# A graph-and-expert kernel on one core: the logits and sums of each chunk of edges split into small steps that run between the picks

## The chip, the cores and the metric

The kernel runs on one core of one Trainium2 chip. The metric is the device time of one execution in microseconds (us), lower is better; runs are given by their median. The engines are TensorE (PE; its weight loads are PEld), VectorE (DVE), ScalarE (ACT), GpSimd (POOL) and SyncE (SP), which here only issues DMAs. Each engine works through its own program in order and waits on semaphores; the shared quantities are SBUF, PSUM (8 banks) and 16 DMA engines.

## The reference, cut to what matters

```python
x = x + gnn(layernorm(x), W, M, src, dst)          # 6250 nodes x 256, 200,000 edges
x = x + ffn(layernorm(x), ...)                      # below
# in ffn: 131,072 edges, HEADS = 4, NUM_EXPERTS = 4, a self loop for each node
h = (x_flat @ W_gat).reshape(M, HEADS, NUM_EXPERTS)
a_src = (h * att_src).sum(-1); a_dst = (h * att_dst).sum(-1)
e = leaky_relu(a_src[src] + a_dst[dst], 0.2)
e_max = segment_max(e, dst); ee = exp(e - e_max[dst]); denom = segment_sum(ee, dst)
agg = segment_sum(h[src] * (ee / denom[dst])[:, :, None], dst)      # 16 numbers a node
scores = layernorm(agg + b_gat).mean over heads; the best 2 of 4 experts gate
out = sum over experts of gate * (gelu(x @ W1[e] + b1[e]) @ W2[e] + b2[e])
```

## The kernel before

The first part (up to about 2230 us) does the first graph layer, sorts the 131,072 edges of the second by destination, and runs most of the experts' matmuls between them. The change lies in the **second edge stage**, about 2269 to 3022 us, and what follows waits for it.

**Edges and chunks.** The sorted edges lie as 1024 columns of 128 partitions, in NCF = 16 chunks of FC = 64 columns. A chunk's buffer `g[:, c % 5]` (GR = 5) holds for each edge 16 features, 4 logits and 4 running maxima. The first PC = 32 columns of a chunk are fetched from `tab_d` by GpSimd: 32 indirect DMAs (L1465), one a column. The other TC = 32 columns are made by TensorE.

**Blocks on TensorE.** 8 blocks (TB) of 4 columns make a chunk's second half, 128 blocks in all. For a block, VectorE writes one-hot rows `low_hot` (L788, 4 instructions; two buffers), TensorE multiplies them with the table in three bf16 parts (L1368, 48 matmuls of 208 columns), and VectorE picks the values out: `picked` (L799) and a reduction into `g` (L804). Block b + 1's one-hot rows wait for block b - 1's matmuls, and TensorE's block b waits for `low_hot` b and for L799 of block b - 2. So TensorE runs at most one block ahead.

**Steps.** `turns_2` sets the order on every engine: "matrix" steps, 4 for each block (516 = 4 x 129 in all), and units of the experts' matmuls that are left (40 of them among the steps: L1314 for a hidden part, L1324 for a y tile, whose bias add L724 is VectorE's). In a block's four steps VectorE does the pick of block b - 1 in the first, the one-hot rows of b + 1 in the second, nothing in the other two.

**Logits and sums.** For chunk c, `weigh(c)` takes the logits: products for the second half (L823, L825), 4 scans that spread the destination's number along the row (L839), a wait for the chunk's 32 gathers (`feat_in`), sum and leaky relu (L846, L847), 4 scans for running maxima (L849), differences (L855 to L858). ScalarE takes exponentials (`exps`). `sum_up(c)` multiplies (L864, L867) and runs 20 scans of 64 columns (L871). In the kernel before, `weigh(c)` runs as a whole after step 32 (c + 1.5) and `sum_up(c)` as a whole after step 32 (c + 1.75). Chunk 15's two run behind the last step.

**GpSimd** runs 32 gathers for chunk 0, 49 scatters of the destinations' numbers into `start_d` (`starts`, L1454), then the gathers of chunks 1 to 15. From chunk 5 on it waits for `summed` of chunk c - 4 and for the store of chunk c - 5.

**SP** waits for all 49 scatters before it loads the first three chunks of `edge` from `start_d` (at step 32), stores a y tile after each y unit, stores a chunk's sums to `sum_d` (L1639) after `sum_up`, and behind the last step issues 15 loads of `comb` (L1676, L1677; 896 KB each) and then the last chunk's sums. When those have landed, GpSimd fetches the rows' last sums (L1473), mends them, and fetches 49 tiles of sums; the gates and the weighted sum of the experts end the kernel.

Of the kernel before, what the change touches and what calls it, by code (L numbers as in the profile page):

```python
# [33 lines left out]
CR = 3  # L34
PART = 3
POOL_TILES = 2


class Steps:
# [16 lines left out]
def sent(k):  # L56

    return 16 * (k + 1)


def build(nc, x, src, dst, W, M, W_gat, att_src, att_dst, b_gat, ln_gamma, ln_beta,
# [3 lines left out]
    NX, _, F = W1.shape  # L65
# [22 lines left out]
    NCF = C2 // FC  # L88
    PC = FC - TC
    NTC = NCF * TC  # L90
    TB = TC // 4
# [194 lines left out]
    def sem(name):  # L286
        if name not in named:
            named[name] = nc.alloc_semaphore(name)
        return named[name]
# [28 lines left out]
    for j in range(V_):  # L318
        paced += PACE if j >= 2 * JC else 0
        n = min(int(paced), sort_total - taken_steps) if j % 2 else 0  # L320
# [35 lines left out]
    for j in range(V_):  # L356
        paced = min(paced + (SEARCH_PACE if search_from <= j <= search_end else UNIT_PACE), 2.0)
        n = 0
        if j % 2 and paced >= 1 and units_1 < len(units):
            what, i, _ = units[units_1]  # L360
            first = y_from if what == "y" else (ready(last_of(jobs[i][0])) + UNIT_WAIT) * JC
            if j >= first:
                n, units_1, paced = 1, units_1 + 1, paced - 1
# [13 lines left out]
    matrix_total = 4 * (NCF * TB + 1)  # L377
# [4 lines left out]
        turns_2 += ["unit"] * int(paced) + ["matrix"]  # L382
        paced -= int(paced)
    turns_2 += ["unit"] * (left - turns_2.count("unit"))
    weigh_at = {int(4 * TB * (c + 1.5)): c for c in range(NCF - 1)}
    sum_at = {int(4 * TB * (c + 1.75)): c for c in range(NCF - 1)}
    low_at = {4 * TB * (c + 1) + 2: c + 2 for c in range(NCF - 2)}

    def vector_program():
        step = Steps(V, dve_step)  # L390

        def then(ins):
            n = step(ins)
            V.wait_ge(dve_step, n)
            return n
# [114 lines left out]
        for b in range(VB + 1):  # L510
# [3 lines left out]
            if b >= 1:  # L514
                V.wait_ge(sem("pairs_turned"), b)
                at = slice((b - 1) * P, b * P)
# [289 lines left out]
        def matrix_gathers():  # L806
            split_table()
            low_columns(0)
            for b in range(NCF * TB + 1):
                if b >= 1:  # L810
                    pick(b - 1)
                yield
                if b + 1 < NCF * TB:
                    low_columns(b + 1)
                yield
                yield
                yield

        def scores(c):

            s = c % GR
            V.wait_ge(dve_step, dve_at["pick", (c + 1) * TB - 1])
            then(V.tensor_tensor(scored[:, :, :], g[:, s, PC:FC, 0:HX],  # L823
                                 attb[:, 0:1, :].broadcast_to([P, TC, HX]), ALU.mult))
            step(V.tensor_reduce(g[:, s, PC:FC, HX:FE], scored[:, :, :].rearrange("p k (h e) -> p k h e", h=HEADS),  # L825
                                 AXX, ALU.add))

        def weigh(c):
            a, b, s, e = c * FC, (c + 1) * FC, c % GR, c % 4
            e_, top_, st = g[:, s, :, HX:FE], g[:, s, :, FE:FG], step_f[:, c % 2, :, :]  # L830
            before_top = None if c == 0 else g[:, (c - 1) % GR, FC - 1:FC, FE:FG]
            a_dest, same = edge[:, e, :, :], same_f[:, a:b]
            scores(c)
            V.wait_ge(sem(f"edge_in{e}"), sent(c // 4))
            if c == 0:
                V.wait_ge(sem("row_in"), 16)
                then(V.tensor_copy(a_dest[:, 0, :], head_row[:, FE:FG]))
            for f in range(HEADS):
                step(V.tensor_tensor_scan(a_dest[:, :, f], same, a_dest[:, :, f],  # L839
                                          0.0 if c == 0 else edge[:, (c - 1) % 4, FC - 1:FC, f], ALU.mult, ALU.add))  # L840
            if c >= 2:
                V.wait_ge(dve_step, dve_at["summed", c - 2])
            step(V.tensor_scalar(reset_c[:, c % 2, :], same, -1.0, BIG, ALU.add, ALU.mult))
            V.wait_ge(sem(f"feat_in{s}"), 16 * PC * (c // GR + 1))
            step.settle()
            then(V.tensor_tensor(e_, e_, a_dest, ALU.add))  # L846
            then(V.scalar_tensor_tensor(out=e_, in0=e_, scalar=0.2, in1=e_, op0=ALU.mult, op1=ALU.max))  # L847
            for h in range(HEADS):
                step(V.tensor_tensor_scan(g[:, s, :, FE + h], reset_c[:, c % 2, :], g[:, s, :, HX + h],  # L849
                                          -BIG if c == 0 else before_top[:, :, h], ALU.add, ALU.max))  # L850
            step.settle()
            if c == 0:
                step(V.memset(st[:, 0:1, :], -BIG))
            else:
                step(V.tensor_tensor(st[:, 0:1, :], before_top, top_[:, 0:1, :], ALU.subtract))  # L855
            step(V.tensor_tensor(st[:, 1:FC, :], top_[:, 0:FC - 1, :], top_[:, 1:FC, :], ALU.subtract))
            then(V.tensor_tensor(e_, e_, top_, ALU.subtract))
            dve_at["weighed", c] = then(V.tensor_scalar(st, st, 0.0, None, ALU.min))  # L858

        def sum_up(c):  # L860
            a, b, s = c * FC, (c + 1) * FC, c % GR
            st = step_f[:, c % 2, :, :]
            V.wait_ge(sem("exps"), c + 1)
            step(V.tensor_tensor(st, st, same_f[:, a:b, None].broadcast_to([P, FC, HEADS]), ALU.mult))  # L864
            for h in range(HEADS):
                o = g[:, s, :, h * NX:(h + 1) * NX]
                step(V.tensor_tensor(o, o, g[:, s, :, HX + h:HX + h + 1].broadcast_to([P, FC, NX]), ALU.mult))  # L867
            step.settle()
            for f in range(FE):
                h = f // NX if f < HX else f - HX  # L870
                step(V.tensor_tensor_scan(g[:, s, :, f], st[:, :, h], g[:, s, :, f],  # L871
                                          0.0 if c == 0 else g[:, (c - 1) % GR, FC - 1:FC, f], ALU.mult, ALU.add))
            dve_at["summed", c] = step.settle()

        matrix_steps, done = matrix_gathers(), 0
        for turn in turns_2:
            if turn == "unit":
                next(mlp)
                continue
            next(matrix_steps)  # L880
            done += 1
            if done in weigh_at:
                weigh(weigh_at[done])
            if done in sum_at:
                sum_up(sum_at[done])
        for _ in mlp:
            pass
        weigh(NCF - 1)

        cm = sm[:, 20:20 + HEADS]  # L890
        w = hm[:, 0, :, :]
        dve_at["tops_spread"] = then(V.tensor_tensor(
            w, ident[:, None, :].broadcast_to([P, HEADS, P]),
            g[:, (NCF - 1) % GR, FC - 1, FE:FG, None].broadcast_to([P, HEADS, P]), ALU.mult))
        sum_up(NCF - 1)
        V.wait_ge(sem("tops_out"), 1)
        then(V.tensor_tensor(w, bank[0][:, :].rearrange("p (h q) -> p h q", h=HEADS),
                             segm[:, 0:1, :].broadcast_to([P, HEADS, P]), ALU.mult))
# [87 lines left out]
        for c in range(NLN):  # L986
# [6 lines left out]
            for e in range(NX):  # L993
                for k in range(XG - POOL_TILES):
                    step(V.scalar_tensor_tensor(  # L995
# [5 lines left out]
    def scalar_program():  # L1001
# [120 lines left out]
        def exps(c):  # L1122
            st, e_ = step_f[:, c % 2, :, :], g[:, c % GR, :, HX:FE]
            A.wait_ge(dve_step, dve_at["weighed", c])
            A.activation(st, st, ACT.Exp)
            A.activation(e_, e_, ACT.Exp).then_inc(sem("exps"), 1)

        done = 0
        for turn in turns_2:
            if turn == "unit":  # L1130
                next(mlp)
                continue
            done += 1
            if done in weigh_at:
                exps(weigh_at[done])
        exps(NCF - 1)
        w = hm[:, 0, :, :]
        A.wait_ge(dve_step, dve_at["carry_logit"])
# [19 lines left out]
        for c in range(NLN):  # L1158
# [5 lines left out]
            for e in range(NX):  # L1164
                for k in range(XG - POOL_TILES, XG):
                    y = comb[:, s, e, k, :]
# [330 lines left out]
    def sync_program():  # L1497
# [78 lines left out]
        for c in range(NCH + AFTER):  # L1576
# [10 lines left out]
            if c == LOW_CH:  # L1587
                Q.wait_ge(dve_step, dve_at["low_rows"])
                for k in range(LB):
                    n = min(P, NTC - k * P)  # L1590
# [17 lines left out]
            if size(c):  # L1608
                n = size(c)
# [12 lines left out]
        def load_edges(c):  # L1622
            if c >= 4:
                Q.wait_ge(dve_step, dve_at["weighed", c - 3])
            Q.dma_start(edge[:, c % 4, :, :].rearrange("p j f -> p (j f)"),
                        start_d.rearrange("(p j) f -> p (j f)", p=P)[:, c * FC * HEADS:(c + 1) * FC * HEADS]
                        ).then_inc(sem(f"edge_in{c % 4}"), 16)
# [9 lines left out]
        def store_sums(c):  # L1637
            Q.wait_ge(dve_step, dve_at["summed", c])
            Q.dma_start(sum_rows[:, c * FC:(c + 1) * FC, :], g[:, c % GR, :, :]).then_inc(sem(f"sum_out{c % GR}"), 16)  # L1639
# [4 lines left out]
        done = 0  # L1644
        for turn in turns_2:
            if turn == "unit":
                next(mlp)
                continue
            done += 1
            if done == 4 * TB:  # L1650
                Q.wait_ge(sem("start_out"), 16 * NT)
                for c in range(3):
                    load_edges(c)
            if done in low_at:
                load_low(low_at[done])
            if done in weigh_at and weigh_at[done] + 3 < NCF:
                load_edges(weigh_at[done] + 3)
            if done in sum_at:
                store_sums(sum_at[done])
        for _ in mlp:  # L1660
            pass
        for k in range(2):
# [19 lines left out]
        for c in range(NLN):  # L1682
# [3 lines left out]
            n = min(XG, FULL // P - c * XG)  # L1686
# [38 lines left out]
```

## Time and profile before

| what | us |
|---|---|
| median of 3 runs | 3240.63 (3239.18 to 3240.84) |
| the profiled execution | 3242.23, its span 3240.9 |
| TensorE's first and last matmul of the stage (L1368) | 2269.2, 3022.0 |
| GpSimd's gathers of chunks 1 to 15 | 2340.4 to 2999.3 |
| first `comb` load issued; last sums landed | 3027.0; 3071.8 |
| from there to the end | 169.1 |

The profile's span is 1.3 us less than the profiled execution's time, and that time is 1.6 us over the median. In the profile each row of a timeline is a run of like instructions on one engine: its start, how long it took, the count, and in brackets for how long the engine was idle before it and what released it.

### The profile page before, as it was taken

How to read it: one execution, taken by the hardware profiler on the slowest of the kernel's cores; microseconds unless marked ns; L12 is line 12 of the kernel's file. 1: busy time of each engine (PE TensorE's matmuls, PEld its weight loads, DVE VectorE, ACT ScalarE, POOL GpSimd, SP SyncE). 2: the span in 40 equal slices, each digit the busy share in tenths (PEclk: the TensorE clock that was granted, in tenths of full speed). 3: DMA queues.
4: the chain of work that ended last, by engine and by line, in shares of the span. 5: the costliest groups of instructions: out<-in, count | busy, mean ns of one | idle time of the engine just before them, and what ended most of it. 6: DMA issues, size and time to landing. Idle time of an engine off the chain costs nothing.

```text
span 3240.9 us, 41199 instructions
## 1 busy us (share of the span) xinstructions
PE 2411.0 (74%) x13096; PEld 1894.9 (58%) x13096; DVE 2192.3 (68%) x5126; ACT 543.2 (17%) x924; POOL 2331.4 (72%) x2315
## 2 busy tenths in 40 slices
PE   1466878878778888788888888886888888888300
PEld 0344555556556555566666666664788887888200
DVE  6488777678685656565556555553588888888568
ACT  4000212112123333211111111111000000000012
POOL 3777777777777777777777777774777777777073
PEclk9777999889889989899999999898999999999655
DMA  8876777667767777777777777774122122211518
GB/s 277 297 226 218 221 224 226 216 214 230 218 208 243 239 223 238 223 223 236 232 247 246 239 235 238 234 237 131 26 62 62 39 61 62 55 44 44 192 43 270
DMA packets 470542, 599.63 MB, mean 185 GB/s; under 512 B 66293, under 2 KB 409270, under 8 KB 468278
## 3 DMA queue, kind: packets, MB, share of 16 engines
q1 hardware_dynamic: 372310, 375.12, 34.9%
q0 software_dynamic: 97568, 220.03, 24.6%
q8 instruction: 105, 1.72, 0.2%
q10 hardware_dynamic: 448, 1.85, 0.2%
q14 instruction: 111, 0.91, 0.1%
HBM read 312.22 MB, written 286.19 MB: 185 GB/s over the span
## 4 chain that ended last, share of the span: by engine, by line
PE 32%; DVE 16%; DMA 9%; issue 6%; POOL 5%; SPq 3%; ACT 1%; DVEq 0%; POOLq 0%; ACTq 0%
PE wide L1266 9%; PE wide L1368 9%; PE wide L1324 5%; PE wide L1314 5%; DMA run_d<-ring 4%; DVE g L871 2%; DMA fetched<-x_d 2%; DVE ring L746 2%; DVE low_hot L788 2%; DVE comb L995 2%; DVE picked L799 2%; PE wide L1283 2%; POOL ring L1438 1%; POOL start_d L1454 1%; DMA ring<-xn_d,srci 1%
## 5 line engine op out<-in xcount | busy, mean ns | idle before, releaser
L1438 POOL DMA_INDIRECT ring<-xn_d,srci x1611 | 1623.4, 1008 | 516.7 <-issue 443.6
L746 DVE SCALAR_TENSOR_TENSOR ring<-ring,same_v,wide 128x256 f32<-128x256 f32 x1610 | 770.6, 479 | 694.8 <-PE wide L1266 588.0
L1266 PE MATMUL wide<-ring,one_hot 128*128 128x256 f32 x3222 | 916.8, 421 | 164.5 <-DVE ring L746 95.1
L1266 PEld LDWEIGHTS wide<-ring,one_hot 128*128 128x128 f32 x3222 | 652.7, 211 | 377.8 <-DVE ring L746 132.6
L1368 PE MATMUL wide<-tab_parts,low_hot 128*128 128x208 bf16 x6144 | 599.9, 263 | 120.2 <-DVE low_hot L788 120.2
L1368 PEld LDWEIGHTS wide<-tab_parts,low_hot 128*128 128x128 bf16 x6144 | 576.4, 102 | 145.5 <-DVE low_hot L788 128.4
L1465 POOL DMA_INDIRECT g<-tab_d,srt x512 | 547.2, 1069 | 156.0 <-issue 154.2
L1324 PE MATMUL wide<-w2s,hh 128*128 128x256 f32 x1568 | 390.1, 394 | 2.3 <-DVE yo L724 2.3
L1314 PE MATMUL wide<-xt,w1s 128*128 128x512 f32 (+1 forms) x832 | 390.8, 594 | 0.8 <-DVE feat L714 0.8
L1324 PEld LDWEIGHTS wide<-w2s,hh 128*128 128x128 f32 x1568 | 311.7, 200 | 56.0 <-issue 6.1
L1079 ACT ACTIVATE hh<-wide,b1c 128x512 f32<-128x512 f32 (+1 forms) x208 | 137.8, 663 | 1218.2 <-PE wide L1314 1217.9
L682 DVE TENSOR_TENSOR one_hot<-iota_f,dloc 128x512 f32<-128x512 f32 x403 | 276.5, 687 | 3.1
L1314 PEld LDWEIGHTS wide<-xt,w1s 128*128 128x128 f32 x832 | 162.4, 202 | 113.5 <-issue 99.1
L799 DVE TENSOR_TENSOR picked<-wide,high_hot 128x832 f32<-128x832 f32 x128 | 130.8, 1022 | 106.7 <-PE wide L1368 105.7
L1274 PE MATMUL wide<-ident,fetched 128*128 128x128 f32 x196 | 46.0, 378 | 182.4 <-DMA fetched<-x_d 182.4
L788 DVE TENSOR_SCALAR low_hot<-low_row,lane 128x512 bf16<-128x512 f16 x512 | 157.0, 369 | 0.0
L1274 PEld LDWEIGHTS wide<-ident,fetched 128*128 128x128 f32 x196 | 29.8, 187 | 205.1 <-DMA fetched<-x_d 204.7
L804 DVE TENSOR_REDUCE g<-picked 128x64 f32<-128x832 f32 x128 | 130.6, 1020 | 4.4
L724 DVE TENSOR_TENSOR yo<-wide,b2b 128x256 f32<-128x256 f32 x196 | 82.0, 418 | 46.8 <-PE wide L1324 45.6
L607 DVE TENSOR_TENSOR keys<-keys 128x512 f32<-128x512 f32 (+1 forms) x198 | 112.2, 567 | 0.0
L606 DVE TENSOR_TENSOR keys<-keys 128x512 f32<-128x512 f32 (+1 forms) x198 | 111.8, 565 | 0.0
L1095 ACT ACTIVATE tin<-wide 128x512 f32<-128x512 f32 x49 | 29.2, 597 | 461.4 <-PE wide L1274 461.4
(332 smaller groups left out, 1569.8 us busy)
## 6 DMA issues: line engine op xcount, KB each, us to landing
run_d<-ring SPq DMA_DIRECT2D x201, 1024.0 KB, 5.3
ring<-xn_d,srci POOLq DMA_INDIRECT x1611
y_d<-yo SPq DMA_DIRECT2D x196, 128.0 KB
comb<-y_d SPq DMA_DIRECT2D x28, 896.0 KB, 9.6
low_row<-low_d SPq DMA_DIRECT2D x16, 1024.0 KB, 5.6
sum_d<-g SPq DMA_DIRECT2D x16, 768.0 KB, 3.3
g<-tab_d,srt POOLq DMA_INDIRECT x512
xn_d<-ring SPq DMA_DIRECT2D x7, 896.0 KB, 5.6
```

What stands on the lines that cost most here:

```text
L682: dve_at["one_hot", b] = step(V.tensor_tensor(one_hot[:, b % 4, 0:n, :], iota_f[:, None, :].broadcast_to([P, n, P]), dloc[:, 4 * b:4 * b + ...
L746: dve_at["run", j] = step(V.scalar_tensor_tensor(out=o, in0=ring[:, (j - 1) // JC % RING, (j - 1) % JC, :], scalar=same_v[:, j:j + 1], in1 ...
L788: dve_at["low_hot", b] = step(V.tensor_scalar(low_hot[:, b % 2, q_, :], low_row[:, c % 2, at:at + LOW], lane[:, q_:q_ + 1], None, ALU.is_e ...
L799: dve_at["taken", b] = then(V.tensor_tensor(picked[:, :, :, :], wide[:, 4 + half:6 + half, :].rearrange("p c (k x) -> p (c k) x", k=2)[:, ...
L804: dve_at["pick", b] = step(V.tensor_reduce(g[:, c % GR, k:k + 4, 0:HX], picked[:, :, :, :], AXX, ALU.add))
L1079: A.activation(hh[:, i % 2, f, 0:n * P], bank[hidden_bank[nl]][:, 0:n * P], ACT.Gelu, bias=b1c[:, e, f:f + 1], scale=1.0).then_inc(sem("ge ...
L1266: T.matmul(wide[:, 4 + j // 2 % 2, j % 2 * D:(j % 2 + 1) * D], one_hot[:, j // 4 % 4, j % 4, :], ring[:, j // JC % RING, j % JC, :], start ...
L1314: mm = T.matmul(bank[hidden_bank[nl]][:, 0:n * P], w1s[:, e, k, f * P:(f + 1) * P], xt[:, c % 2, k, 0:n * P], start=(k == 0), stop=(k == K ...
L1324: mm = T.matmul(bank[y_bank[ny]][:, 0:D], hh[:, i % 2, k, f * P:(f + 1) * P], w2s[:, e, k, :], start=(k == 0), stop=(k == KF - 1))
L1368: mm = T.matmul(bank[4 + 2 * (b % 2) + i // 2][:, at:at + HX * HI], low_hot[:, b % 2, q_, i * P:(i + 1) * P], tab_parts[:, k, q_, :, :].re ...
L1438: G.indirect_dma_start(out=ring[:, s, j % JC, :], out_offset=None, in_=xn_d, in_offset=at_rows(srci[:, j:j + 1])).then_inc(sem(f"gather{s} ...
L1465: G.indirect_dma_start(out=g[:, s, k, :], out_offset=None, in_=tab_d, in_offset=at_rows(srt[:, j:j + 1])).then_inc(sem(f"feat_in{s}"), 16)
```

## The change

`weigh` and `sum_up` become generators. `weigh(c)` yields 9 times and `sum_up(c)` 13 times; the 20 scans are in 10 pieces of 2. A new generator, `chunk_steps`, runs through chunks 0 to 14 with 29 steps each (CHUNK_STEPS): 9 for the logits, 4 empty ones, 13 for the sums, 3 empty ones. From step 89 on (first_weigh = 88) each matrix step of VectorE advances it by one. The instructions, their number and their operands stay the same. Chunk 0's logits so begin 40 steps later than before, chunk 14's at step 495 where it was 496. The last steps of chunk 14's sums lie behind step 516, and run ahead of chunk 15. ScalarE's exponentials, SP's loads of `edge` and its stores of sums move with them; SP's wait for the scatters moves from step 32 to step 84, and chunk 14's store behind its loop.

```diff
+CHUNK_STEPS = 29
+WEIGH_STEPS = 9
+EXP_STEPS = 4
+SUMMED_STEPS = 28
...
-    weigh_at = {int(4 * TB * (c + 1.5)): c for c in range(NCF - 1)}
-    sum_at = {int(4 * TB * (c + 1.75)): c for c in range(NCF - 1)}
+    first_weigh = 4 * TB * 11 // 4
+    weighed_at = {first_weigh + CHUNK_STEPS * c + WEIGH_STEPS: c for c in range(NCF - 1)}
+    summed_at = {first_weigh + CHUNK_STEPS * c + SUMMED_STEPS: c for c in range(NCF - 1)}
...
             for f in range(HEADS):
                 step(V.tensor_tensor_scan(a_dest[:, :, f], same, a_dest[:, :, f],
                                           0.0 if c == 0 else edge[:, (c - 1) % 4, FC - 1:FC, f], ALU.mult, ALU.add))
+                if f % 2:
+                    yield
...
             for h in range(HEADS):
+                if h % 2 == 0:
+                    yield
                 step(V.tensor_tensor_scan(g[:, s, :, FE + h], reset_c[:, c % 2, :], g[:, s, :, HX + h],
...
             for f in range(FE):
+                if f % 2 == 0:
+                    yield
                 h = f // NX if f < HX else f - HX
                 step(V.tensor_tensor_scan(g[:, s, :, f], st[:, :, h], g[:, s, :, f],
                                           0.0 if c == 0 else g[:, (c - 1) % GR, FC - 1:FC, f], ALU.mult, ALU.add))
             dve_at["summed", c] = step.settle()
-
-        matrix_steps, done = matrix_gathers(), 0
+            yield
+
+        def chunk_steps():
+
+            for c in range(NCF - 1):
+                n = 0
+                for _ in weigh(c):
+                    n += 1
+                    yield
+                assert n <= WEIGH_STEPS
+                for _ in range(WEIGH_STEPS + EXP_STEPS - n):
+                    yield
+                n = WEIGH_STEPS + EXP_STEPS
+                for _ in sum_up(c):
+                    n += 1
+                    yield
+                assert n <= SUMMED_STEPS
+                for _ in range(CHUNK_STEPS - n):
+                    yield
...
             next(matrix_steps)
             done += 1
-            if done in weigh_at:
-                weigh(weigh_at[done])
-            if done in sum_at:
-                sum_up(sum_at[done])
+            if done > first_weigh:
+                next(chunks, None)
         for _ in mlp:
             pass
-        weigh(NCF - 1)
+        for _ in chunks:
+            pass
+        for _ in weigh(NCF - 1):
+            pass
...
-            if done == 4 * TB:
+            if done == first_weigh - 4:
                 Q.wait_ge(sem("start_out"), 16 * NT)
                 for c in range(3):
                     load_edges(c)
...
-            if done in weigh_at and weigh_at[done] + 3 < NCF:
-                load_edges(weigh_at[done] + 3)
-            if done in sum_at:
-                store_sums(sum_at[done])
+            if done in weighed_at and weighed_at[done] + 3 < NCF:
+                load_edges(weighed_at[done] + 3)
+            if done in summed_at:
+                store_sums(summed_at[done])
+        for at, c in summed_at.items():
+            if at > matrix_total:
+                store_sums(c)
```

VectorE in the middle of the stage, one chunk's sums, before: L799, L804 and L788 are a block's pick and one-hot rows, L864, L867 and L871 the sums (the scans are printed as SCALAR_TENSOR_TENSOR here).

```order
L799 TENSOR_TENSOR picked<-wide,high_hot 128x832
L804 TENSOR_REDUCE g<-picked 128x4x16
L788 TENSOR_SCALAR low_hot<-low_row,lane 128x512 x4
L864 TENSOR_TENSOR step_f<-step_f,same_f 128x256
L867 TENSOR_TENSOR g<-g 128x64x4 x4
L871 SCALAR_TENSOR_TENSOR g<-step_f,g 128x64 x20
L799 TENSOR_TENSOR picked<-wide,high_hot 128x832
```

The same place now; the line numbers are those of the changed kernel (L805, L810 and L794 are the pick and the one-hot rows, L879, L885 and L891 the sums).

```order
L794 TENSOR_SCALAR low_hot<-low_row,lane 128x512 x4
L891 SCALAR_TENSOR_TENSOR g<-step_f,g 128x64 x6
L805 TENSOR_TENSOR picked<-wide,high_hot 128x832
L810 TENSOR_REDUCE g<-picked 128x4x16
L891 SCALAR_TENSOR_TENSOR g<-step_f,g 128x64 x2
L794 TENSOR_SCALAR low_hot<-low_row,lane 128x512 x4
L891 SCALAR_TENSOR_TENSOR g<-step_f,g 128x64 x6
```

The 25 instructions of the sums stood together between two blocks; now at most 6 scans stand between two instructions of a block.

SP, the first loads of `edge` (L1625) among the loads of `low_row` (L1632), the first sums (L1639) and the y tiles (L1571), before:

```order
L1571 DMA y_d<-yo 128x256
L1625 DMA edge<-start_d 128x256 x3
L1632 DMA low_row<-low_d 128x4096
L1625 DMA edge<-start_d 128x256
L1570 TENSOR_LOAD tiles_i
L1570 ISA x2
L1571 ISA
L1571 DMA y_d<-yo 128x256
L1639 DMA sum_d<-g 128x1536
```

And now (L1666, L1673, L1680 and L1612 are the same four):

```order
L1612 DMA y_d<-yo 128x256
L1673 DMA low_row<-low_d 128x4096
L1611 TENSOR_LOAD tiles_i
L1611 ISA x2
L1612 ISA
L1612 DMA y_d<-yo 128x256
L1666 DMA edge<-start_d 128x256 x4
L1673 DMA low_row<-low_d 128x4096
```

The loads of `edge`, which stand behind the wait for the scatters, moved behind two loads of `low_row` and two y tiles.

## Rows read from the trace of the kernel before

**Rows 1.** The page: busy time of each engine, and the gathers' group.

```profile
PE 2411.0 (74%) x13096; PEld 1894.9 (58%) x13096; DVE 2192.3 (68%) x5126; ACT 543.2 (17%) x924; POOL 2331.4 (72%) x2315
...
L1465 POOL DMA_INDIRECT g<-tab_d,srt x512 | 547.2, 1069 | 156.0 <-issue 154.2
```

**Rows 2.** Busy time by stretch; then PEclk, DMA share and GB/s.

```profile
2397.80:2401.20 3.40, 3.40 (x23) 3.01 (x21) 3.37 (x9) 0.00 (x0) 2.54 (x3) 0.51 0.10 11
2343.60:3022.00 678.40, 579.40 (x5713) 551.50 (x5714) 565.67 (x1335) 59.34 (x82) 510.37 (x478) 0.92 0.22 54
```

**Rows 3.** Waits in the stage: us in total, times, longest.

```profile
PE wide L1368 <- DVE low_hot L788: 120.2, 31, 16.6
DVE picked L799 <- PE wide L1368: 105.7, 66, 6.3
```

**Rows 4.** Timeline of TensorE around chunk 1's logits and sums.

```profile
2370.48 14.07 PE L1368 MATMUL wide<-tab_parts,low_hot 128*128 128x208 bf16 x156
2384.39 1.91 PE L1324 MATMUL wide<-w2s,hh 128*128 128x256 f32 x8
2386.14 7.65 PE L1368 MATMUL wide<-tab_parts,low_hot 128*128 128x208 bf16 x84
2396.92 8.25 PE L1368 MATMUL wide<-tab_parts,low_hot 128*128 128x208 bf16 x72 [3.13 <-DVE low_hot L788]
```

**Rows 5.** Timeline of VectorE, chunk 1's logits, sums and next blocks.

```profile
2387.72 0.68 DVE L823 TENSOR_TENSOR scored<-g,attb 128x512 f32<-128x512 f32 x1
...
2393.41 0.29 DVE L858 TENSOR_SCALAR step_f<-step_f 128x256 f32<-128x256 f32 x1
2393.74 1.02 DVE L799 TENSOR_TENSOR picked<-wide,high_hot 128x832 f32<-128x832 f32 x1
...
2400.00 0.47 DVE L864 TENSOR_TENSOR step_f<-step_f,same_f 128x256 f32<-128x256 f32 x1
...
2401.84 5.82 DVE L871 TENSOR_TENSOR_SCAN g<-step_f,g 128x64 f32<-128x64 f32 x20
2407.70 1.02 DVE L799 TENSOR_TENSOR picked<-wide,high_hot 128x832 f32<-128x832 f32 x1
2408.76 1.02 DVE L804 TENSOR_REDUCE g<-picked 128x64 f32<-128x832 f32 x1
...
2410.74 1.02 DVE L799 TENSOR_TENSOR picked<-wide,high_hot 128x832 f32<-128x832 f32 x1
```

**Rows 6.** Timeline of GpSimd over the same scans.

```profile
2402.59 1.02 POOL L1465 DMA_INDIRECT g<-tab_d,srt  x1 [0.30 <-issue]
2403.92 4.57 POOL L1465 DMA_INDIRECT g<-tab_d,srt  x1 [0.30 <-issue]
2408.80 0.94 POOL L1465 DMA_INDIRECT g<-tab_d,srt  x1 [0.30 <-issue]
2410.05 1.07 POOL L1465 DMA_INDIRECT g<-tab_d,srt  x1 [0.30 <-issue]
```

**Rows 7.** Timeline of GpSimd, over the start of chunk 8's sums.

```profile
2728.09 1.84 POOL L1465 DMA_INDIRECT g<-tab_d,srt  x1 [0.31 <-issue]
```

**Rows 8.** Timeline of GpSimd: last scatter, first and last gather of chunks 1 to 15, fetch.

```profile
2339.16 0.98 POOL L1454 DMA_INDIRECT start_d<-feat,idx_s  x1 [0.30 <-issue]
2340.44 1.00 POOL L1465 DMA_INDIRECT g<-tab_d,srt  x1 [0.31 <-issue]
...
2998.26 1.07 POOL L1465 DMA_INDIRECT g<-tab_d,srt  x1 [0.30 <-issue]
3071.82 0.94 POOL L1473 DMA_INDIRECT sm<-sum_d,smi  x1 [72.49 <-DMA sum_d<-g]
```

**Rows 9.** Timeline of VectorE: chunk 0's logits.

```profile
2343.56 0.40 DVE L837 COPY edge<-head_row 128x4 f32<-128x4 f32 x1 [14.55 <-DMA edge<-start_d]
```

**Rows 10.** Timeline of SP's queue behind the last block.

```profile
3027.01 4.75 SPq L1676 DMA_DIRECT2D comb<-y_d  x4
...
3060.66 2.54 SPq L1639 DMA_DIRECT2D sum_d<-g  x1
```

More of the change, by code:

```diff
@@ L384, in build @@
     turns_2 += ["unit"] * (left - turns_2.count("unit"))
-    weigh_at = {int(4 * TB * (c + 1.5)): c for c in range(NCF - 1)}
-    sum_at = {int(4 * TB * (c + 1.75)): c for c in range(NCF - 1)}
+    first_weigh = 4 * TB * 11 // 4
+    weighed_at = {first_weigh + CHUNK_STEPS * c + WEIGH_STEPS: c for c in range(NCF - 1)}
+    summed_at = {first_weigh + CHUNK_STEPS * c + SUMMED_STEPS: c for c in range(NCF - 1)}
+    assert first_weigh + CHUNK_STEPS * (NCF - 2) + WEIGH_STEPS < matrix_total
     low_at = {4 * TB * (c + 1) + 2: c + 2 for c in range(NCF - 2)}
@@ L864, in sum_up @@
             step(V.tensor_tensor(st, st, same_f[:, a:b, None].broadcast_to([P, FC, HEADS]), ALU.mult))
+            yield
             for h in range(HEADS):
+                if h == 2:
+                    yield
                 o = g[:, s, :, h * NX:(h + 1) * NX]
@@ L869, in sum_up @@
             for f in range(FE):
+                if f % 2 == 0:
+                    yield
                 h = f // NX if f < HX else f - HX
@@ L873, in sum_up @@
             dve_at["summed", c] = step.settle()
-        matrix_steps, done = matrix_gathers(), 0
+            yield
+        def chunk_steps():
[3 more added lines that the diff above has]
+                    n += 1
+                    yield
+                assert n <= WEIGH_STEPS
+                for _ in range(WEIGH_STEPS + EXP_STEPS - n):
+                    yield
+                n = WEIGH_STEPS + EXP_STEPS
+                for _ in sum_up(c):
+                    n += 1
+                    yield
+                assert n <= SUMMED_STEPS
+                for _ in range(CHUNK_STEPS - n):
+                    yield
+        matrix_steps, chunks, done = matrix_gathers(), chunk_steps(), 0
         for turn in turns_2:
@@ L894, in vector_program @@
             g[:, (NCF - 1) % GR, FC - 1, FE:FG, None].broadcast_to([P, HEADS, P]), ALU.mult))
-        sum_up(NCF - 1)
+        for _ in sum_up(NCF - 1):
+            pass
         V.wait_ge(sem("tops_out"), 1)
@@ L1133, in scalar_program @@
             done += 1
-            if done in weigh_at:
-                exps(weigh_at[done])
+            if done in weighed_at:
+                exps(weighed_at[done])
         exps(NCF - 1)
```

## The prediction

> **What bounds the kernel now.** I read the page first: over the whole span no engine is full, TensorE is busy 74% of it, VectorE 68%, GpSimd 72% [rows 1], so the stage has to be read by itself. In the stage TensorE needs 13.91 us for 156 matmuls (14.07 with the last one's own length; the next matmuls start at 2384.39) [rows 4], that is 4.28 us for a block's 48. VectorE needs 3.04 us for a block's pick and one-hot rows (2407.70 to 2410.74) [rows 5]. So between the chunks' work TensorE sets the pace and VectorE has 1.24 us to spare in a block, which is why the picks wait for TensorE 105.7 us in all [rows 3]. Then come the logits, 6.02 us in one piece (2387.72 to 2393.74), and the sums, 7.70 us in one piece (2400.00 to 2407.70) [rows 5]. TensorE runs at most one block ahead, so each piece stops it: 31 waits for the one-hot rows, 120.2 us in all, 3.9 us on average, 16.6 the longest [rows 3]. The longest is chunk 0's, whose logits wait 14.55 us for the first `edge` load behind the 49 scatters [rows 9]. A stop also costs clock: after one of 3.13 us [rows 4] a stretch of 3.4 us was granted 0.51 of the clock, the lower of its two levels (1.2 of 2.4 GHz), and held 23 matmuls [rows 2], where at full level 38 would fit. Over the stage the clock is 0.92 [rows 2].
>
> The second bound lies close behind. GpSimd never waits in this stage, but for 0.3 us of issue before each gather (156.0 over 512 [rows 1]): its gathers of chunks 1 to 15 run from 2340.44 to 2999.3 [rows 8], 658.9 us or 43.9 a chunk. Its pitch without trouble is 1.25 us a gather (2408.80 to 2410.05 [rows 6]), 40.0 a chunk; so 3.9 a chunk are delays, 3.6 of them in one gather. That one stands in every chunk's 20 scans: 4.57 us where 0.94 is usual, and it ends 0.83 us behind the last scan [rows 5, 6]. Before, a chunk's 32 steps took about 47 us, more than GpSimd's 43.9, so its rows were always there in time. TensorE's last matmul ended at 3022.0, GpSimd at 2999.3: only 22.7 us lie between them.
>
> Last, the way out. Behind the last block SP issues the `comb` loads from 3027.01, its queue takes the last sums at 3060.66, and they have landed at 3071.82, when GpSimd goes on [rows 8, 10]: 44.8 us from first load to landing. All of the remaining 169.1 us follow from there.
>
> **The change part by part.** *What goes.* With at most 6 scans between two of a block's instructions, TensorE's waits shrink. Per interval of 29 steps (7.25 blocks) TensorE needs 7.25 x 4.28 = 31.0 us and its share of the 40 units (0.31 a block, 1.76 us each from 2384.39 to 2386.14 [rows 4]: 3.9), 34.9 in all. VectorE needs 7.25 x 3.04 + 6.02 + 7.70 = 35.8. Since the pieces stand in 22 of 29 steps, VectorE is a little late there and idle elsewhere; I take 37 us. Without GpSimd the steps would cost 37 a chunk.
>
> *What is late next.* GpSimd needs 40 + x a chunk, x being its delays, which is more than 37. Step 88 comes at about 2269 + 22 blocks x 4.8 us (4.28 and the units) = 2375, chunk 0's logits then find edges and rows there, and its 14.55 us wait is gone. From there the steps reach chunk c's logits at 2378 + 37 c, while its gathers are there at 2340 + (40 + x) c + 2. For x near 1.3 the two cross at chunk 8; from then on VectorE waits inside the logits for the gathers, in front of the picks and one-hot rows that are queued behind that wait, and TensorE waits for those. So the pace is GpSimd's, and the end is computed from it.
>
> *The sum.* x: the small delays of today, 43.9 - 40 - 3.5 = 0.4, stay. The long one depends on how scans keep GpSimd out. The gather that starts 0.75 us into the 20 scans takes 1.02 us, 0.08 too much; only the one that starts 2.08 us in is caught [rows 5, 6]. Six scans last 1.73 us (5.82 less 5.82/20 for each left out), so runs of the new length lie wholly in the part that lets gathers through. Against this stands one gather of 1.84 us near a start of the sums [rows 7], 0.9 too much, which I found in 3 of the 14 chunks with smaller ones. I price each of a chunk's three or four runs at 0.08 plus a fifth of 0.9, some 0.9 together, and take x = 1.3.
> Gathers of chunk 14 are then there at 2340.4 + 14 x 41.3 + 2 = 2920.6. From its fourth logit step VectorE still has 18 steps, 4.5 blocks x 3.04 = 13.7 us, and 3.7 us of logits and 7.7 of sums: 25 us, so its sums end at 2946. SP can then issue the `comb` loads at about 2947, and one store of sums (2.5 us in the queue [rows 10]) stands ahead of them. The last sums land at 2947 + 2.5 + 44.8 = 2994.3, against 3071.8: 77.5 us less. Chunk 15 is hidden: its gathers are there at 2340.4 + 15 x 41.3 + 2 = 2961.9, logits, spread and sums take 12 to 13 us more, 2975, and the queue reaches its store only at 2983. The rest is unchanged. The profiled execution's 3242.2 less 77.5 is 3164.7; the median stands 1.6 below that execution, so 3163.
>
> *Costed at nothing.* No instruction is added. ScalarE's exponentials have four empty steps (over 4 us) for 0.8 us of work. SP's wait for the scatters (the last starts at 2339.16 [rows 8]) is moved to step 84, at about 2370, past two `low_row` loads and two y stores, which it no longer holds up. Chunk 5's gathers wait for chunk 1's sums at about 2440, and start at 2505. If any of these covers failed, the price would be a stop such as those of today, 3.9 us each.
>
> *A rule.* The scans read two SBUF operands. Back to back, they let two gathers through at 1.02 us and then none [rows 6]. The Trainium skill (SBUF — State Buffer, Who interferes with whom) says that a VectorE instruction with two SBUF inputs contends with a GpSimd instruction that reads SBUF, as a lock for the whole instruction; taken at its word each piece of scans could hold up a gather wherever it stands, which is the third rival below.
>
> **The rivals.** (1) *The same starvation.* The scans' total is the same, and the low_hot instructions beside them may count as part of a run. Then x stays 3.9: chunk 14's gathers are there 2.6 x 14 = 36.4 us later, 3200. The ends of the long gather, 4.57, at any chunk [rows 6] speak for a fixed amount of blocking; the two that pass speak against it.
> (2) *VectorE stays the bound.* If pieces between picks cost as many stops as before, the steps keep some 45 us a chunk and only the first wait (14.55) goes: about 3225. Against it: the sum of VectorE's work is 35.8.
> (3) *Slower: every piece of scans catches a gather*, as in the 1.84 us row [rows 7]. Ten pieces at 0.9 make x = 9.4; the last sums land 8.1 x 14 = 113 us later than in my sum, 3277. It decides from x = 1.3 + 77.5/14 = 6.8 on, 0.64 us for each piece. Against it stand the gathers that pass between scans [rows 6].
> (4) *Slower: the clock.* TensorE's waits become short and frequent. If it stood at the lower level for half of the blocks, a block would cost the mean of 4.28 and twice that, 6.4 us, 129 blocks and 70 us of units 896 against 753 now, some 140 slower, 3380. The dip shown follows a stop of 3.1 us, and such stops become rare, against it.
>
> **How the numbers follow.** My forecast has 63%, and by itself x from 0.4 to about 2.5: 3150 to 3180, with 5 us for gathers that land later while the `comb` loads fill the DMA engines. Rival 1 has 20% (3180 to 3212), rival 2 6%, rival 3 7%, rival 4 4%. The range 3145 to 3210 takes in most of the first two. A measurement of this kernel tells 0.2%, 6.5 us, from no change. Faster by more: 0.88; within: 0.03; slower: 0.09.
>
> **What the profile would show.** Right: no gather over 2 us in the scans, GpSimd's last gather of the stage near 2960, waits of VectorE inside the logits (the sum of g and edge, L846 before) that begin at about chunk 8, TensorE's waits more in number and mostly under 2 us, the first `comb` load near 2950 and the fetch of the last sums near 2994, 169 us before the end. Rival 1 shows in the gathers' end at 2999 and waits for gathers from chunk 1 or 2 on. Wrong altogether would be gathers of 1.8 us at every piece, or a mean clock under 0.8 in the stage.

## The result, and the profile after

The changed kernel takes **3158.17 us** (median of 4 runs, 3153.76 to 3162.35) where the kernel before takes 3240.74 (4 runs): a ratio of 0.9745, interval 0.9728 to 0.9762, some 82.6 us less. The profiled execution took 3162.35, its span is 3161.0. L805, L810, L794, L1409, L1506 are what L799, L804, L788, L1368, L1465 were.

The page's two groups of the stage, TensorE's matmuls and GpSimd's gathers (count, busy us, mean ns, idle before and its releaser), against 599.9 busy and 120.2 waited on TensorE, and the 547.2 of [rows 1]:

```profile
L1409 PE MATMUL wide<-tab_parts,low_hot 128*128 128x208 bf16 x6144 | 573.3, 255 | 62.2 <-DVE low_hot L794 61.8
L1506 POOL DMA_INDIRECT g<-tab_d,srt x512 | 506.4, 989 | 156.1 <-issue 153.6
```

The stage, first matmul 2269.8 to last 2934.7, is 664.9 us long where it was 752.8. Busy time of each engine from chunk 0's old stop on, and then PEclk, against [rows 2], where that stretch had 0.92:

```profile
2343.60:2934.70 591.10, 541.23 (x5622) 515.83 (x5620) 549.12 (x1301) 60.63 (x83) 451.06 (x460) 0.99 0.24 59
```

The waits in the stage, against [rows 3]:

```profile
PE wide L1409 <- DVE low_hot L794: 61.8, 47, 12.4
...
DVE picked L805 <- PE wide L1409: 39.2, 28, 6.3
...
DVE g L855 <- DMA g<-tab_d,srt: 14.5, 6, 4.6
```

TensorE waits for the one-hot rows more often and for less: 61.8 us here, 58.4 less. 12.4 of it, as of the 120.2 before, is the wait for the stage's very first rows. The picks wait 39 us for TensorE, no longer 106: VectorE is now the busier of the two (549 of 591 us). New is the last line, VectorE inside the logits waiting for gathers. The rest of the gain is the matmuls themselves, 599.9 to 573.3 us busy, 26.6 less, since the clock of the stretch is 0.99: behind its first microseconds it falls only after the four stops of 2.5 to 4.9 us, where before it fell after most of the stops. 58.4 and 26.6 are 85 of the stage's 87.9.

GpSimd, first and last gather of chunks 1 to 15 and the fetch of the last sums, against [rows 8]:

```profile
2341.13 1.00 POOL L1506 DMA_INDIRECT g<-tab_d,srt  x1 [0.30 <-issue]
...
2958.22 0.94 POOL L1506 DMA_INDIRECT g<-tab_d,srt  x1 [0.30 <-issue]
2992.72 0.94 POOL L1514 DMA_INDIRECT sm<-sum_d,smi  x1 [33.56 <-DMA sum_d<-g]
```

618.1 us for 15 chunks, 41.2 each where it was 43.9. SP behind the last block, against [rows 10]:

```profile
2942.11 0.32 SPq L1680 DMA_DIRECT2D sum_d<-g  x1
2942.75 6.44 SPq L1720 DMA_DIRECT2D comb<-y_d  x4
...
2981.69 2.54 SPq L1680 DMA_DIRECT2D sum_d<-g  x1
```

Chunk 14's sums are stored at 2942.11, `comb` follows at once, and the fetch comes at 2992.72, 168 us before the span's end (it was 169).

### The profile page after: what moved, and what is told of

Its sections match the earlier page's. It is cut to its first block and busy times, and to the rows that moved or that the text cites. A ratio compares the mean times of both kernels' runs of the same rounds, so it can differ in the third digit from the quotient of the medians.

```text
span 3161.0 us, 41206 instructions
## 1 busy us (share of the span) xinstructions
PE 2382.3 (75%) x13096; PEld 1866.7 (59%) x13096; DVE 2190.1 (69%) x5126; ACT 543.4 (17%) x924; POOL 2290.7 (72%) x2315
## 5 line engine op out<-in xcount | busy, mean ns | idle before, releaser
L1409 PE MATMUL wide<-tab_parts,low_hot 128*128 128x208 bf16 x6144 | 573.3, 255 | 62.2 <-DVE low_hot L794 61.8
L1506 POOL DMA_INDIRECT g<-tab_d,srt x512 | 506.4, 989 | 156.1 <-issue 153.6
L1409 PEld LDWEIGHTS wide<-tab_parts,low_hot 128*128 128x128 bf16 x6144 | 551.8, 99 | 85.4 <-DVE low_hot L794 75.4
L1315 PE MATMUL wide<-ident,fetched 128*128 128x128 f32 x196 | 44.8, 370 | 176.1 <-DMA fetched<-x_d 176.1
L805 DVE TENSOR_TENSOR picked<-wide,high_hot 128x832 f32<-128x832 f32 x128 | 130.3, 1018 | 40.3 <-PE wide L1409 39.2
L794 DVE TENSOR_SCALAR low_hot<-low_row,lane 128x512 bf16<-128x512 f16 x512 | 157.5, 369 | 0.8
L810 DVE TENSOR_REDUCE g<-picked 128x64 f32<-128x832 f32 x128 | 130.6, 1020 | 4.4
```

The lines of the kernel that those rows point to most:

```text
L794: dve_at["low_hot", b] = step(V.tensor_scalar(low_hot[:, b % 2, q_, :], low_row[:, c % 2, at:at + LOW], lane[:, q_:q_ + 1], None, ALU.is_e ...
L805: dve_at["taken", b] = then(V.tensor_tensor(picked[:, :, :, :], wide[:, 4 + half:6 + half, :].rearrange("p c (k x) -> p (c k) x", k=2)[:, ...
L810: dve_at["pick", b] = step(V.tensor_reduce(g[:, c % GR, k:k + 4, 0:HX], picked[:, :, :, :], AXX, ALU.add))
L1409: mm = T.matmul(bank[4 + 2 * (b % 2) + i // 2][:, at:at + HX * HI], low_hot[:, b % 2, q_, i * P:(i + 1) * P], tab_parts[:, k, q_, :, :].re ...
L1506: G.indirect_dma_start(out=g[:, s, k, :], out_offset=None, in_=tab_d, in_offset=at_rows(srt[:, j:j + 1])).then_inc(sem(f"feat_in{s}"), 16)
```

## The experiments

But for the chip at the end of this section, the runs are from chips where the kernel before takes 3240 to 3242 us (medians); the medians of the changed kernels are of 4 or 5 runs.

**1. The 20 scans whole.** Everything stays split and moved but the scans.

```diff
             for f in range(FE):
-                if f % 2 == 0:
+                if f == 0:
                     yield
```

> The changed kernel with one part undone: the 20 scans of a chunk's sums stand in one piece again; all else stays split. Theory A (GpSimd's gathers set the end of the stage, and a run of 20 scans starves them): one gather of about 4.5 us a chunk comes back, the gathers of chunks 1 to 15 take about 43.9 us a chunk instead of 41.2, chunk 14's are there about 38 us later, and the time is about 3195 (3185 to 3205). Theory B (the pace is set by TensorE and VectorE; GpSimd is not the limit): only one more stop of TensorE of about 4 us a chunk, partly made up in the empty steps, at most 3175.

Measured: 3206.2 us (ratio 0.9886, 0.9862 to 0.991), 1 us above Theory A's range and far from Theory B's. GpSimd's gathers of the 15 chunks (busy us, mean ns), and one of the long ones, which are there again in each chunk from 1 on:

```profile
L1506 POOL DMA_INDIRECT g<-tab_d,srt x480 | 513.1, 1069 | 146.3 <-issue 143.8 <-DVE picked L805 0.6 <-DVE g L891 0.6
```

```profile
2608.76 4.58 POOL L1506 DMA_INDIRECT g<-tab_d,srt  x1 [0.30 <-issue]
```

They end at 3000.3, 43.9 a chunk, and the fetch of the last sums comes at 3034.62, 42 us later than in the changed kernel. So 10 pieces of two scans instead of one of 20 are worth about 48 of the 83 us.

The time is Theory A's, but the wait is not. VectorE's timeline shows no wait for gathers in chunks 1 to 14: its logits take up chunk 14's gathers 5.3 us after they have ended, without a pause.

```profile
2955.29 0.94 POOL L1506 DMA_INDIRECT g<-tab_d,srt  x1 [0.30 <-issue]
```

```profile
2961.56 0.44 DVE L855 TENSOR_TENSOR g<-g,edge 128x256 f32<-128x256 f32 x1
```

The steps themselves had become slower, as Theory B has it: the sums of chunks 0 to 14 end 41.1 us apart. The stage is 704.5 us long against 664.9, and of these 39.6 us TensorE's waits for the one-hot rows make 25.7 (87.5 against 61.8) and its matmuls 13.1 (586.4 us busy against 573.3, at a clock of 0.95 against 0.98 over the whole stage). But chunk 14's gathers end 38.7 us later than in the changed kernel, which waits for them, so faster steps alone would have won back at most some 4 us. The two limits lie that close together here, and this run can't say how much of the 48 us is due to either. The whole scans without the scatters would tell; that was not run.

**2. Moved but not split.**

```diff
-                n = 0
-                for _ in weigh(c):
-                    n += 1
-                    yield
-                assert n <= WEIGH_STEPS
-                for _ in range(WEIGH_STEPS + EXP_STEPS - n):
-                    yield
-                n = WEIGH_STEPS + EXP_STEPS
-                for _ in sum_up(c):
-                    n += 1
-                    yield
+                for _ in range(WEIGH_STEPS - 1):
+                    yield
+                for _ in weigh(c):
+                    pass
+                yield
+                for _ in range(EXP_STEPS + 12):
+                    yield
+                for _ in sum_up(c):
+                    pass
+                yield
+                n = WEIGH_STEPS + EXP_STEPS + 13
```

> The changed kernel with the logits and the sums of a chunk each in one piece again, but at the new places (29 steps a chunk, the logits at the ninth of them, the first at step 97). It tells the moving from the splitting. Theory A (the splitting carries the gain; moving takes only chunk 0's wait of 14.55 us away): TensorE's waits for the one-hot rows stay near 105 us, time 3220 to 3240. Theory B (the late start carries it): about 3175.

Measured: 3276.46 us (ratio 1.01, 1.0078 to 1.0121). Both theories missed: moving alone is not worth little, it costs 34 us. Its waits, and its longest stop but the first in TensorE's timeline:

```profile
PE wide L1409 <- DVE low_hot L794: 140.3, 30, 12.4
```

```profile
2559.96 4.33 PE L1409 MATMUL wide<-tab_parts,low_hot 128*128 128x208 bf16 x24 [6.62 <-DVE low_hot L794]
```

And what VectorE did before that, from the reduction of a pick to the next one-hot rows:

```profile
2550.16 1.02 DVE L810 TENSOR_REDUCE g<-picked 128x64 f32<-128x832 f32 x1
2551.10 0.41 DVE L879 TENSOR_TENSOR step_f<-step_f,same_f 128x256 f32<-128x256 f32 x1
2551.43 1.42 DVE L885 TENSOR_TENSOR g<-g 128x256 f32<-128x256 f32 x4
2552.89 5.82 DVE L891 TENSOR_TENSOR_SCAN g<-step_f,g 128x64 f32<-128x64 f32 x20
2558.75 1.16 DVE L794 TENSOR_SCALAR low_hot<-low_row,lane 128x512 bf16<-128x512 f16 x4
```

The sums stand between a block's pick and its one-hot rows, since 29 steps are no multiple of 4: TensorE, one block ahead at most, waits for nearly all of the 7.7 us. Chunk 0's long wait is gone, but the 29 stops behind the very first cost 4.4 us on average; in the kernel before the 29 stops other than the very first and chunk 0's cost 3.1.

**3. The same with 28 steps a chunk**, each piece behind a fourth step.

```diff
-CHUNK_STEPS = 29
+CHUNK_STEPS = 28
-SUMMED_STEPS = 28
+SUMMED_STEPS = 25
-    first_weigh = 4 * TB * 11 // 4
+    first_weigh = 4 * TB * 11 // 4 + 3
-                for _ in range(EXP_STEPS + 12):
+                for _ in range(EXP_STEPS + 11):
-                n = WEIGH_STEPS + EXP_STEPS + 13
+                n = WEIGH_STEPS + EXP_STEPS + 12
```

> whole_late (logits and sums each in one piece at new places, 3276 us, where 3220 to 3240 had been expected) with 28 steps a chunk instead of 29, so that every piece stands behind a block's fourth step as in the kernel before, the first at step 100. Theory A (in whole_late the pieces wander through the block's steps, and one that stands behind the first step, between the pick and the one-hot rows, costs TensorE 5.0 to 6.6 us where the others cost 2.5 to 4): no stop over 5.2 us behind the first, stops of 3.5 us on average as before, 105 to 110 us in all, time 3235 to 3260. Theory B (what costs is that two pieces come every 29 steps instead of every 32, at a time when nothing else is different): 3275 or more.

Measured: 3254.99 us (ratio 1.005, 1.0031 to 1.0068), 21 less than in experiment 2, within Theory A's time but not with its stops. Its waits are

```profile
PE wide L1409 <- DVE low_hot L794: 127.5, 30, 12.4
```

115.1 us in 29 stops behind the first, 4.0 each, five of them at 5.4 to 5.9, where none over 5.2 was expected. So the place in the block is part of the matter (4.4 to 4.0, none at 6.6 any more), but not all: 3.5 was expected, and the kernel before has 3.1. Why whole pieces cost more here than where they stood before stays open.

**4. Split but not moved.**

```diff
-CHUNK_STEPS = 29
+CHUNK_STEPS = 32
-    first_weigh = 4 * TB * 11 // 4
+    first_weigh = 4 * TB * 3 // 2 - 1
-            if done == first_weigh - 4:
+            if done == 4 * TB:
```

> The changed kernel with the splitting alone: chunk 0's logits begin at step 48 as in the kernel before, 32 steps a chunk, the loads of edge behind the wait for the scatters at step 32 again. Theory A (the stage's end is set by chunk 14's gathers, which don't depend on when the logits begin): chunk 0's wait of about 12 to 15 us comes back but is made up before chunk 11, time 3155 to 3165. Theory B (the late start is worth its wait): about 3172.

Measured: 3165.64 us (ratio 0.977, 0.9743 to 0.9797; the changed kernel's interval, 0.9728 to 0.9762, overlaps it), just above Theory A's range. The waits:

```profile
PE wide L1409 <- DVE low_hot L794: 67.4, 51, 12.4
...
DVE g L855 <- DMA g<-tab_d,srt: 12.6, 6, 3.6
DVE edge L844 <- DMA edge<-start_d: 12.6, 1, 12.6
```

Chunk 0's wait for the first edges is back, 12.6 us, and the waits for gathers are 12.6 where they were 14.5: from the middle of the stage both kernels wait for the same gathers. In its profiled execution the first matmul is at 2263.5 and the fetch of the last sums at 2989.56, 726.1 us later; in the changed kernel 722.9. So the late start with 29 steps a chunk instead of 32 brings 3 us in the traces, up to 7 in the medians, not told from none, and the splitting carries the rest.

**5. Without the scatters.** It leaves out the destinations' share of the logits.

```diff
-            for t in range(NT):
-                G.indirect_dma_start(out=start_d, out_offset=at_rows(idx_s[:, t:t + 1]), in_=feat[:, t, FE:FG],
-                                     in_offset=None, bounds_check=E2 - 1,
-                                     oob_is_err=False).then_inc(sem("start_out"), 16)
...
-                Q.wait_ge(sem("start_out"), 16 * NT)
```

> The changed kernel without GpSimd's 49 scatters of the destinations' numbers into start_d (that part of the computation is left out: the destinations' share of the logits is zero but for a row's head). GpSimd has 63 us less to do ahead of chunk 1's gathers. Theory A (from about chunk 11 on the stage waits for GpSimd): VectorE's waits for gathers vanish, the steps keep 37 us a chunk to the end, chunk 14's sums end about 20 us earlier, time 3130 to 3142. Theory B (TensorE and VectorE set the pace to the end): 3155 to 3160 as with the scatters.

Measured: 3133.44 us (ratio 0.9665, 0.964 to 0.969), Theory A. No wait for gathers is left and TensorE's are

```profile
PE wide L1409 <- DVE low_hot L794: 49.7, 49, 12.4
```

with chunk 14's sums stored at 2917.79 and a granted clock of 1.00 over the stage (behind its first microseconds no stretch at the lower level). The changed kernel is thus held some 25 us by GpSimd; here, with the gathers begun 68 us earlier, the sums end 36.4 us apart up to chunk 14.

**6. Two runs of ten scans**, a block apart.

```diff
             for f in range(FE):
-                if f % 2 == 0:
+                if f == 0:
                     yield
+                if f == 10:
+                    for _ in range(4):
+                        yield
```

> The changed kernel with the 20 scans in two runs of 10 (2.9 us each), a block apart. Theory A (in runs of 20 the first two gathers passed and only one that started over 1.8 us in was caught, until the end): longest gathers about 1.7 us where the 20 gave 4.6, 41 to 42 us for a chunk's gathers, time 3160 to 3175. Theory B (a lock held in proportion to the scans' total time, whatever their runs): 43 us and more a chunk, 3190.

Measured: 3180.52 us (ratio 0.9816, 0.9795 to 0.9836), between the times of the two theories. Gathers take 42.9 a chunk (chunks 1 to 14, 2335.8 to 2936.7) and 9 of them 3.1 us. One of these, and VectorE around it:

```profile
2439.60 0.94 POOL L1509 DMA_INDIRECT g<-tab_d,srt  x1 [0.31 <-issue]
2440.85 3.10 POOL L1509 DMA_INDIRECT g<-tab_d,srt  x1 [0.30 <-issue]
2444.26 0.94 POOL L1509 DMA_INDIRECT g<-tab_d,srt  x1 [0.30 <-issue]
```

```profile
2438.19 1.02 DVE L810 TENSOR_REDUCE g<-picked 128x64 f32<-128x832 f32 x1
2439.12 1.13 DVE L794 TENSOR_SCALAR low_hot<-low_row,lane 128x512 bf16<-128x512 f16 x4
2440.17 2.96 DVE L894 TENSOR_TENSOR_SCAN g<-step_f,g 128x64 f32<-128x64 f32 x10
2443.16 1.02 DVE L805 TENSOR_TENSOR picked<-wide,high_hot 128x832 f32<-128x832 f32 x1
```

The gather starts only 0.68 us into the scans, where I had expected it to pass, but 1.73 us after the start of the four one-hot instructions, which the scans follow without a gap. It ends 0.82 us behind the last scan. I looked at the gathers over 1.3 us behind the scatters, of this trace (24) and of the changed kernel's (7): each started 1.7 to 2.7 us after the start of such an unbroken run of one-hot, product and scan instructions, and ended 0.8 us behind the run, whether a pick ended it or VectorE's pause of some 0.04 us between the products and the scans. So the one-hot instructions ahead of the scans count too, and the length of the scans alone doesn't tell.

But a start that late is not enough. Of the gathers that started 1.7 us or more into such a run, with 0.5 us or more of it left, 24 of 35 were held here, and only 7 of 37 in the changed kernel; the others took at most 1.3 us. Here is one that passed, 2.34 us into a run of the same 4 one-hot instructions and 10 scans, with 1.69 us of it left:

```profile
2435.54 1.08 POOL L1509 DMA_INDIRECT g<-tab_d,srt  x1 [0.30 <-issue]
```

```profile
2433.20 1.15 DVE L794 TENSOR_SCALAR low_hot<-low_row,lane 128x512 bf16<-128x512 f16 x4
2434.28 2.95 DVE L894 TENSOR_TENSOR_SCAN g<-step_f,g 128x64 f32<-128x64 f32 x10
```

What tells the held ones from those that pass is open, and so is what it is in a pick or a pause that lets a held gather go. All this is read from traces; none of it was tried by itself.

**7. The last sums before the third group of `comb`.**

```diff
-        for c in range(CR):
+        for c in range(CR - 1):
             load_comb(c)
         store_sums(NCF - 1)
+        load_comb(CR - 1)
```

> The changed kernel as the measure for tail_b in this call, since the call before it ran on a chip where TensorE was fed one matmul in 2.8 us for stretches of the trace: 3155 to 3165 if this chip is like the first.

> The changed kernel, but SP issues two groups of comb loads, then the last chunk's sums, then the third group. Theory A (the store's landing behind the comb loads sets the rest): it lands 8 to 9 us earlier than in the changed kernel (2991.8 in its first trace), and the time is 8 to 9 us less than after_b. Theory B (the third group of loads is needed as early, or the store shares the queue anyway): within 2 us of after_b. On the slow chip the order gave 4347 against 4376, too far apart in its stalls to be read.

Measured on one chip: the changed kernel 3158.47 us (5 runs, 3145.77 to 3161.48), the other order 3152.1 (5 runs, 3150.92 to 3161.05; ratio to the kernel before 0.974 and 0.9743, with intervals of 0.002 to each side). It is the fastest median of a kernel that computes all, and not told from the changed kernel. GpSimd from the fetch of the last sums to the first of the 49 fetches, first in the changed kernel (its sums were made at 2961.4), then in the other (2969.9):

```profile
2978.16 0.94 POOL L1514 DMA_INDIRECT sm<-sum_d,smi  x1 [33.31 <-DMA sum_d<-g]
2982.87 1.02 POOL L1517 DMA_INDIRECT sum_d<-sm,smi  x1 [3.77 <-DVE sm L960]
2985.29 0.97 POOL L1522 DMA_INDIRECT fsum<-sum_d,idx_f  x1 [1.40 <-DMA sum_d<-sm,smi]
```

```profile
2975.32 0.94 POOL L1514 DMA_INDIRECT sm<-sum_d,smi  x1 [22.62 <-DMA sum_d<-g]
2983.30 1.02 POOL L1517 DMA_INDIRECT sum_d<-sm,smi  x1 [7.03 <-DVE sm L960]
2988.18 0.97 POOL L1522 DMA_INDIRECT fsum<-sum_d,idx_f  x1 [3.87 <-DMA sum_d<-sm,smi]
```

The sums land 5.4 us after they are made, no longer 16.8; but from there to the first of the 49 fetches it is 12.9 us instead of 7.1, for the two small DMAs now run beside the third group: the DMA engines are 100% busy in these 12.9 us and 3% in the other kernel's 7.1. Of some 11 us won, half is given back. Theory A's earlier landing is there, but the medians lie only 6.4 us apart, and the runs of the two kernels overlap, so no gain is shown.

**Another chip.** The same order, the ten-scan kernel and the order with a later start also ran on a slower chip:

> tail_order with the logits begun 8 steps later (first_weigh 96). Theory A (the steps wait for GpSimd from about chunk 11 on, so a later start lets TensorE finish first): TensorE's last matmul about 8 us earlier, but the last chunk's sums hang on GpSimd's last gather as before, so the time is within 2 us of tail_order. Theory B (the lag costs, since more sums stand behind the last step): 3 to 6 us slower than tail_order.

On that chip the kernel before took 4459 us, the changed kernel 4376, this one 4359, the other order alone 4347, the ten-scan kernel 4391. For the changed kernel I had expected the time of the first chip, 3155 to 3162. Its ratio there is 0.9807 (0.976 to 0.9853), so it is faster there too. For stretches of over 100 us TensorE started one matmul in 2.80 us, though nothing in the profile held it:

```profile
3016.83 0.33 PE L1409 MATMUL wide<-tab_parts,low_hot 128*128 128x208 bf16 x1 [2.47 <-issue]
3019.63 0.33 PE L1409 MATMUL wide<-tab_parts,low_hot 128*128 128x208 bf16 x1 [2.47 <-issue]
```

The idle time put down to issue before L1409 is 424.1 us there. The runs of one kernel lie up to 55 us apart there, so differences of a few us between kernels mean nothing, and whether a later lag still helps stays open.

## Why the prediction was right, step by step

Predicted 3163, measured 3158.2.

- **TensorE's stops** shrink as forecast: mostly about 1 us, 45 with the first, the longest behind it 4.9. That VectorE's and TensorE's own pace would be 37 us a chunk was right: the sums of chunks 0 to 9 end at 2413.5 to 2747.2, 37.1 each; without the scatters the steps keep it to the end (36.4).
- **What is late next** was named rightly. GpSimd's 41.3 a chunk were 41.2; VectorE waits for gathers in the logits from chunk 9 on, where chunk 8 had been worked out. Experiment 5 shows it: 25 us earlier with gathers begun 68 us earlier. Experiment 1, with slower gathers, ends 42 us later but shows it only in part, since there the steps themselves are as slow.
- **The sum**, term by term: chunk 14's rows there at 2920.6, measured 2919.1 (the start of the instruction that waits for them); its sums' end at 2946, measured 2942.1; the first `comb` load at 2947, measured 2942.8; the landing at 2994.3, measured 2992.7. That the last agrees so well is partly luck: the store ahead of the loads held the queue for 0.6 us and not 2.5, and from the first load to the landing it was 50.0 us and not 44.8. Of the 5 us between 3163 and 3158.2, 2.6 are the profiled execution against the median: it lay 1.6 above the median before and 4.2 above it now.
- **x = 1.3**, the one term that was chosen and not read, was 1.2, for a partly wrong reason. I had argued that six scans are too short a run. But six gathers of chunks 1 to 14 took 1.34 to 1.95 us, each from 1.7 us on into an unbroken run that the one-hot instructions lengthen (experiment 6). These long ones cost 0.3 us a chunk, about half of what I had given them, and the small delays of the others 0.9, where I had 0.7: two errors that cancel. Why they stayed so few is open, for 30 of the 37 gathers that started that late in a run passed.
- **The clock** was in the sum only as a pace of 4.28 us a block, and it should have been named as a gain: 26.6 us of the stage's 87.9.
- **Rival 1** (3200) did not come; experiment 1 (3206) brings back its gathers of 43.9 us a chunk and its time, but not its waits, as said there. **Rival 3** did not come either: seven gathers over 1.3 us stand against 150 pieces of two scans in chunks 0 to 14. The Trainium skill's rule (SBUF — State Buffer, Who interferes with whom), a lock for the length of each instruction with two SBUF inputs, agrees with these traces only in that VectorE can hold up a gather; a lock for one scan would last 0.3 us, but the held gathers waited for the whole run to end, and most gathers beside such instructions were not held at all. **Rivals 2 and 4** did not come: the steps took 37 us a chunk and not 45, GpSimd was the limit in the last third, and the clock rose.
- **Costed at nothing**: the moved wait for the scatters did cost nothing. That the start could be moved at no loss was right, that it brings chunk 0's wait (12 to 15 us) is shown by experiment 4 to be mostly hollow, since GpSimd takes it back.

## What to carry to other kernels

Before a stall is taken out, ask which engine comes next and what its own rate is: here GpSimd's gathers took 43.9 us a chunk behind a stage of 47. At that rate chunk 14's end 38.7 us later (experiment 1), so by them alone nearly half of the gain could not have come, had the same edit not also freed them. Work for an engine that feeds another through a buffer one block deep did best here in pieces about as long as its slack in a block (1.24 us here), and behind the instruction that the other waits for. A time that is met does not show the mechanism: experiment 1 had Theory A's time with Theory B's slower steps, and only the waits told. And moving whole pieces without splitting them can lose (34 us in experiment 2, 21 of them won back in experiment 3 by the place within the block).

## What the runs showed of the hardware

- A gather issued from GpSimd beside VectorE instructions on SBUF operands took 0.94 to 1.3 us or was held until 0.8 us after the end of an unbroken run of them. In the traces of the kernel before, the changed kernel and experiment 6 all 48 that took over 1.3 us had started 1.7 to 2.7 us into such a run, but many that started as late passed (30 of 37 in the changed kernel). Runs of 5.8 us gave gathers of 4.3 to 4.9, runs of 4.0 us up to 3.1, runs of 2.9 to 3.4 us up to 2.0.
- TensorE's clock: with stops of mostly 1.6 to 5.0 us its granted clock was 0.92 over the stage; with stops of mostly about 1 us it was 0.99, falling to its lower level only after four of 2.5 to 4.9; and 1.00 where none over 1.4 us came behind the first (without the scatters).
- One chip started one matmul in 2.80 us for stretches, with no wait that the profile shows, and the kernel before took 4459 us there instead of 3241.
